# Reading a step's eight tile numbers at its beginning instead of one ahead of each addition of sums

## What is computed

```python
scores = jnp.einsum('ehd,ehd->eh', q[dst], k[src] + ep[:, None, :]) * scale
scores = scores * ew[:, None]
m = jax.ops.segment_max(scores, dst, num_segments=n)
ex = jnp.exp(scores - m[dst])
s = jax.ops.segment_sum(ex, dst, num_segments=n)
attn = ex / s[dst]
out = jax.ops.segment_sum(attn[:, :, None] * v[src], dst, num_segments=n)
```

## Time and profile before

| | us |
|---|---|
| median of three runs | 4696.7 |
| the profiled execution | 4699.27 |
| its span | 4697.5 |
| edge pass, from the first copy of indices in the loop (2342.0) to the last (4013.7), 49 steps | 1671.7 |

### The profile page before, as it was taken

How to read it: one execution, slowest core, us unless ns; L and a number is a source line. 1 busy time by engine, 2 the same in 40 slices (tenths; PEclk the granted TensorE clock), 3 DMA queues, 4 the chain that set the end, 5 groups by cost and what they waited for, 6 DMA issues and landing times. The chain is left out here.

```text
span 4697.5 us, 64474 instructions
## 1 busy us (share of the span) xinstructions
PE 3211.3 (68%) x12643; PEld 2346.8 (50%) x12644; DVE 2496.5 (53%) x5566; ACT 1568.2 (33%) x3419; POOL 1926.7 (41%) x1857
## 2 busy tenths in 40 slices
PE   1577777777673991674477777777777777449594
PEld 1466566556341781342255555555555555336463
DVE  4443333333251004347587877877777777761314
ACT  0333333333320230141244444444444444222221
POOL 1777777777104004000545445454545454220001
PEclk9677777777785995786688888988888898669797
DMA  3755555555101662300555555554555555200000
GB/s 92 203 145 145 144 144 143 141 144 139 29 1 56 199 210 79 121 13 12 155 136 148 142 138 150 139 146 132 151 139 140 149 142 145 97 23 0 18 0 30
DMA packets 339646, 525.74 MB, mean 112 GB/s; under 512 B 169022, under 2 KB 229962, under 8 KB 335696
## 3 DMA queue, kind: packets, MB, share of 16 engines
q0 software_dynamic: 114432, 353.45, 27.3%
q1 hardware_dynamic: 224892, 170.78, 13.3%
q10 hardware_dynamic: 260, 0.80, 0.0%
HBM read 462.21 MB, written 63.83 MB: 112 GB/s over the span
## 5 line engine op out<-in xcount | busy, mean ns | idle before, releaser
L2187 POOL DMA_INDIRECT store<-kv_d,flash_index x832 | 869.8, 1045 | 888.3 <-PE flash_sums L2231 644.4
L717 POOL DMA_INDIRECT agg_rows<-xn_d,agg_index x832 | 795.1, 956 | 320.7 <-issue 224.2
L810 PE MATMUL agg_sums<-agg_rows,agg_member 128*128 128x257 f32 x1664 | 577.3, 508 | 230.2 <-ACT agg_rows L730 130.5
L2220 PE MATMUL flash_query<-q,flash_mem_t 128*128 x1664 | 501.2, 453 | 239.3 <-DVE store L2392 93.6
L810 PEld LDWEIGHTS agg_sums<-agg_rows,agg_member 128*128 128x128 f32 x1664 | 403.4, 257 | 384.8 <-ACT agg_rows L730 272.2
L730 ACT ACTIVATE agg_rows<-agg_rows,weight_of 128x256 f32<-128x256 f32 x832 | 369.9, 500 | 640.7 <-DMA agg_rows<-xn_d,agg_index 638.3
L2231 PE MATMUL flash_sums<-store,flash_member 128*128 128x264 f32 x1664 | 460.3, 423 | 174.8 <-DVE acc L2465 144.5
L2220 PEld LDWEIGHTS flash_query<-q,flash_mem_t 128*128 128x128 f32 x1664 | 344.8, 225 | 336.2 <-issue 281.5
L786 DVE TENSOR_TENSOR acc<-acc,agg_sums 128x257 f32 x416 | 176.5, 424 | 589.5 <-PE agg_sums L810 539.8
L2231 PEld LDWEIGHTS flash_sums<-store,flash_member 128*128 128x128 f32 x1664 | 322.3, 205 | 296.1 <-DVE acc L2465 131.3
L2305 ACT ACTIVATE flash_mem_t<-flash_wide,minus_row 128x512 f32<-128x512 f32 x208 | 142.9, 687 | 574.2 <-PE flash_wide L2209 574.2
(11 more groups left out here) (398 smaller groups left out, 4698.4 us busy)
## 6 DMA issues: line engine op xcount, KB each, us to landing
expert_w<-in_L_ffn_W_dram SPq DMA_DIRECT2D x64, 512.0 KB, 4.5
agg_feats<-in_ef_t_dram SPq DMA_DIRECT2D x52, 512.0 KB, 6.9
agg_rows<-xn_d,agg_index POOLq DMA_INDIRECT x832, 2.8
ep_d<-agg_ep SPq DMA_DIRECT2D x52, 256.0 KB
store<-kv_d,flash_index POOLq DMA_INDIRECT x832, 3.8
flash_ep<-ep_d SPq DMA_DIRECT2D x416, 32.0 KB
flash_flags<-flags_d SPq DMA_DIRECT2D x416, 32.0 KB
xs_d<-zeros SPq DMA_DIRECT2D x1, 8448.0 KB, 30.9
```

Source lines behind the costliest of these rows:

```text
L717: pool.indirect_dma_start(rows[:, q, 0:D], None, sh.xn_d, bass.IndirectOffsetOnAxis(ap=index[:, q:q + 1], axis=0)).then_inc(gathered[u], 16)
L810: last = pe.matmul(sums[:, u % 4, 0:W], member[:, u % WI * SUBS + k, :], rows[:, q, :], start=(k == 0), stop=(k == SUBS - 1))
L2187: pool.indirect_dma_start(ring[:, s, :], None, sh.kv_d, bass.IndirectOffsetOnAxis(ap=index[:, s:s + 1], axis=0)).then_inc(gathered[p][g], 16)
L2220: last = pe.matmul(query[:, c * D:(c + 1) * D], mem_t[:, g % 2, c * P:(c + 1) * P], sh.q[:, bass.ds(t, 1), :], start=True, stop=True)
```

## The change

The reads of the tile numbers go from `keep` and `rescale` to the beginning of a body. The drains, the waits and the additions stay where they are. `rescale` takes the first of the eight values and has no read of its own, so there are eight reads a step instead of nine.

```diff
-                def rescale(a):
-                    t = dve.value_load(sh.tile_id[0:1, bass.ds(WI * a.at, 1)], min_val=0, max_val=NT - 1)
+                def rescale(a, tiles):
+                    t = tiles[0]
                     dve.drain()
                     dve.wait_ge(exp_ready, a.at + 2)
...
-                def keep(a, g):
+                def keep(a, g, tiles):
                     for n in range(2):
-                        t = dve.value_load(sh.tile_id[0:1, bass.ds(WI * a.at + (2 * g + n), 1)], min_val=0, max_val=NT - 1)
+                        t = tiles[2 * g + n]
                         dve.drain()
                         dve.wait_ge(sums_done, WI * a.at + (2 * WI + 2 * g + n + 1))
...
                 def body(s, a, ffn):
+                    if a is not None:
+                        tiles = [dve.value_load(sh.tile_id[0:1, bass.ds(WI * a.at + n, 1)], min_val=0, max_val=NT - 1)
+                                 for n in range(WI)]
                     if a is not None and s is not None:
                         dve.tensor_copy(index[:, a.side * WS:(a.side + 1) * WS], sh.src_of[:, bass.ds(WS * s.at + WS, WS)]
                                         ).then_inc(index_ready, 1)
```

More of the change, by code:

```diff
@@ L2490, in body @@
                     if a is not None:
-                        rescale(a)
+                        rescale(a, tiles)
                         weigh(a, 0)
@@ L2496, in body @@
                         weigh(a, 1)
-                        keep(a, 0)
+                        keep(a, 0, tiles)
                     if s is not None:
@@ L2503, in body @@
                         weigh(a, 2)
-                        keep(a, 1)
+                        keep(a, 1, tiles)
                         weigh(a, 3)
-                        keep(a, 2)
+                        keep(a, 2, tiles)
                     if ffn is not None and ffn[1] == 1:
@@ L2512, in body @@
                     if a is not None:
-                        keep(a, 3)
+                        keep(a, 3, tiles)
                 windows(dve, body)
```

## The result

The changed kernel takes 4960.6 us (median of 4 runs, 4959.7 to 4962.4) against 4698.6 us before (4 runs): 1.056 times as long, 95% interval 1.054 to 1.058. The forecast was 4954.

A forecast was written before the change was run, and what follows sets the result against it. The prediction took DVE's order of work to bound the step. Eight reads (+ 5.6 us), removed reads (- 1.25) and TensorE's lower clock (+ 0.55) made + 4.9 us a step, 255 us over 52 bodies: 4954 us, range 4900 to 5025.

The forecast's parts named there:

- The price of a read, 0.70 us: DVE's sequencer: one register read, address, load, value and check with hops, takes 0.70 us; bounds 0.57 and 0.97.
- The head term: Between a step's last addition and the copy of indices: eight serial reads add 5.6 us a step; bounds 4.6 and 7.8.
- Nothing covers the reads at the head: Head of a step: only the one addition in flight, 0.43 us, runs beside the reads, and that overlap is already spent.
- What the removal gives, 1.25 us: At five additions with only an addition in front, removing reads saves 1.25 us a step; from 0.56 to 1.7.
- The lower clock, + 0.55 us: PE's longer idle at the head puts the second queries at the lower clock: 0.55 us a step; bounds 0 and 1.6.
- The sum: Per step + 5.6 - 1.25 + 0.55 = + 4.9 us; over 52 bodies 255 us, giving 4954 us.
- The range: Time of the changed kernel from 4900 to 5025 us, said to take in the forecast's bounds and the first rival.
- The lowest and the highest case: Lowest 5.6 - 1.7 + 0 = 3.9 us a step, 4900 us; highest 5.6 - 0.8 + 1.6 = 6.4 us, 5030 us.
- Overlapping loads: Rival at the head: the eight loads overlap, a read costs 0.40 us, + 2.25 us a step, 4814 us; chance 0.06.
- the edit that does nothing: Rival: the program keeps each read next to its use or reads again there; 4697 us; chance 0.03.
- The faster case: Rival: reads at the head lie beside queued work or an existing wait, only the gain remains, 4632 us; chance 0.04.
- The deeper fall of the clock: Rival: PE's clock falls further, each step like the one at 0.81, + 5.95 us a step, 5006 us; chance 0.13.

The follow-up runs named there:

- the kernel with one read: Kernel before with only the read ahead of `rescale`, its value addressing all eight additions (computation changed): 4622.1 us, 0.983 of the kernel before.
- the kernel with both sets of reads: Kernel before with eight reads added at the beginning of a body, the old reads ahead of the additions kept: 5028.7 us, 1.066 times the kernel before.
- the half dose: Changed kernel with only four tile numbers read at the beginning, the other four ahead of their additions: 4850.4 us, 1.031 times the kernel before.
- the spread reads: Changed kernel with its eight reads spread to places where DVE's sequencer waits for a long instruction: 4688.3 us, 0.9973 of the kernel before.
- the changed kernel's form with repeated queries: Changed kernel in which PE makes the first queries of a step three times over: 1.046 times the kernel before at 5429.8 us; run again 4963.9 us, 1.056.
- the same idle work in three pauses: Kernel before with PE multiplying the identity 3, 6 and 8 times in three pauses of a step, results unread: 4650.4 us, 0.990 of the kernel before.

## Why the prediction was right, point by point

- **The price of a read, 0.70 us.** Right. Four reads at the head make 2.75 us of pause and eight make 5.60. The head term was + 5.6 us and measured + 5.52, since the 0.08 us that were there before are part of the pause.
- **Nothing covers the reads at the head.** Right: the copy's pause is the reads, whole; the one addition in flight gave nothing, as its time was spent already.
- **What the removal gives, 1.25 us.** Too large: 0.89 us in the changed kernel. The "issue" part fell by 0.61 us a step, a third of it and not the "over half" that was forecast, and the PE part by 0.28. Addition by addition (idle time ahead of each, mean of the 49 steps) the error is at the tail. The second additions of `keep(0)` and `keep(1)` gave 0.51 us together, forecast 0.56. The first additions of `keep(0)`, `keep(1)` and `keep(2)`, whose reads were covered, gave 0.04 us together, forecast nothing. The last three gave 0.34 us, forecast 0.70: the second of `keep(2)` lost 0.49 us, and the last two got 0.15 us longer, waiting for PE. The prediction saw that PE's sums end last there; it kept 0.70 us because DVE's sequencer could hand the last addition over early. No gain of that kind shows in the head's pause. The 1.26 us of the kernel with one read do not support the forecast of 1.25: that kernel also spared the address arithmetic, so the agreement is in part chance.
- **The lower clock, + 0.55 us.** Right in place and near in size: the queries' waits rose by 0.44 us a step, and the second queries are slow in every step. What was argued too simply is that this term belongs to the change's own pause. In other kernels of this study that have no idle work the same waits were 0.8 to 2.4 us, and with four reads at the head they were larger than with eight. Which queries meet the lower clock depends on more than the head: it differs between executions of one kernel too (65 us in the kernel with both sets of reads). In that kernel the waits were 0.8 us a step above those of the changed kernel, 40 us, with the same reads at the head; the range had room for that.
- **The sum.** + 4.9 us a step forecast, + 5.10 measured. The errors are - 0.08 at the head, + 0.36 at the removal, - 0.11 at the clock and + 0.03 for what was not counted. That the time came within 7 us of 4954 is owed in part to their opposite signs; the size of the effect is owed to the head, which was right by itself.
- **The range.** It is looser in its making than it looks. The lowest and the highest case both take the head at 5.6 us, though the text bounds it by 4.6 and 7.8; the highest takes 0.8 us for the removal where the text's own lowest is 0.56, which would give 6.6 us and 5044; and 5025 does not take in the 5030 that was worked out. None of this mattered, as the head's price held.
- **The rivals.** Overlapping loads and the edit that does nothing are excluded by the reads' records at L2469 and by the half dose. The faster case needed reads at 0.16 us; they cost 0.70. The deeper fall of the clock did not come in the changed kernel, but came in the one that keeps both sets of reads: 2.43 us of waits for queries.

What stays open: what the removed reads give by themselves, with addresses kept and PE at one clock, and how much of the 262 us the clock makes in all. With PE kept at work at the head it was 20 us. With PE kept at work in three pauses the kernel before gained 49 us; the changed kernel was not run with all three.

## What to carry to other kernels

In this kernel a read of a register from memory is work of DVE's sequencer, 0.70 us each, one after the other, and what it costs depends on what the engine is executing meanwhile. Eight reads gathered at a place without cover cost their full price, 5.6 us a step; the same eight behind long instructions left no pause of their own. Where one engine's pauses are shortened, look at who ends the wait next: of 0.9 us a step of "issue" pauses that the spread reads removed, 0.5 came back as waits for PE's sums and 0.3 as waits for its queries. Only the waits for queries went away when idle matmuls kept TensorE's clock up. And a control that is to remove one thing should be looked through for what else it removes: here, with the reads, the address arithmetic went.

## What was not expected of the hardware

At one time the kernel before took 5429.8 us instead of 4700, and the changed kernel's form with repeated queries 5679.0 us. In the trace of the latter the records of DVE's sequencer at the eight reads, ns (least, median, most), in one step are:

```profile
L2469 DVEq FUSED_REGOPS  x16: 3/190/1408, 3020.1 to 3033.6; - x16
L2469 DVEq TENSOR_LOAD <-tile_id x8: 3/304/709, 3020.2 to 3033.3; - x8
L2469 DVEq SEQ_ASSERT  x8: 3/23/709, 3020.8 to 3033.9; - x8
```

Eight reads take 13.8 us there instead of 5.6: the medians are those of the other runs, but some records last 709 or 1408 ns. The pause ahead of the copy was 13.4 us on average, against 5.6 us when the same kernel ran again (5.60 us, 4963.9 us). That is 7.8 of the 8.4 us by which its step was longer. What delays the records was not found out; the time of the kernel before varied by 1.2% then, against 0.2% at the other times.

With the same idle work in three pauses, the kernel before ran at a granted clock of 0.96 over the pass and was 1% faster: 1700 matmul records more, which compute nothing, paid for themselves.
